# Splitting the first query/key stage, issuing stack slots singly, and a re-costed static schedule in a fused attention and mixture-of-experts layer

## The reference

```python
q, k, v = x @ Wq, x @ Wk, x @ Wv            # 16 heads of 8
q, k = rope(q), rope(k)
attn = softmax(where(causal, q @ k.T / sqrt(8), -inf)) @ v
x = layernorm(x + attn @ Wo)
# the experts: 8, of which each token takes the best 2; hidden width 256
rw, sel = top_k(x @ router_w.T + bias, 2);  rw = softmax(rw)
y = sum over the two of rw * (silu(x @ w1[e]) * (x @ w3[e])) @ w2[e]
y = y + (silu(x @ sw1) * (x @ sw3)) @ sw2   # the shared expert
out = layernorm(x + y)
```

## Time and profile before

| what | value |
|---|---|
| median of 3 runs | 689.45 us (682.46 to 692.08) |
| the profiled execution's own time | 689.81 us |
| its span | 687.8 us |
| mean granted TensorE clock | 0.885 of full |
| TensorE busy (matmul) | 545.5 us, 79% of the span |
| VectorE busy | 466.5 us, 68% |
| ScalarE, GpSimd busy | 317.6 us (46%), 321.1 us (47%) |

### The profile page before, as it was taken

One profiled execution on the slowest core, in us unless ns is written; L12 is line 12 of the kernel. 1 busy time (PEld: TensorE's weight loads), 2 busy tenths in 40 slices (PEclk: granted clock), 3 DMA queues, 4 the chain that ended last, 5 costly groups with the idle time before them and its releaser, 6 DMA issues.

```text
span 687.8 us, 14778 instructions
## 1 busy us (share of the span) xinstructions
PE 545.5 (79%) x4363; PEld 369.8 (54%) x4363; DVE 466.5 (68%) x1957; ACT 317.6 (46%) x771; POOL 321.1 (47%) x530
## 2 busy tenths in 40 slices
PE   5456888889787999987877979977978997777640
PEld 3111345347265757753555647754766876677640
DVE  3495899989676888756666998756577534753522
ACT  3103875665364676445633666336453582223220
POOL 4303733644871263277753363276462735552313
PEclk9765999999998999898987999897999999878885
DMA  5681322034227636352663536250756585538531
GB/s 150 173 267 42 102 72 71 3 118 125 92 84 220 194 102 194 94 173 80 185 157 116 151 98 193 75 173 28 210 155 188 170 230 151 153 102 249 178 114 40
DMA packets 80063, 94.09 MB, mean 137 GB/s; under 512 B 10224, under 2 KB 61168, under 8 KB 79984
## 3 DMA queue, kind: packets, MB, share of 16 engines
q1 hardware_dynamic: 75888, 84.75, 42.3%
q0 software_dynamic: 4096, 8.40, 3.7%
HBM read 70.37 MB, written 22.35 MB: 135 GB/s over the span
## 4 chain that ended last, share of the span: by engine, by line
PE 40%; DVE 15%; issue 12%; another core or an unknown queue 8%; DMA 7%; POOL 6%; SPq 6%; ACT 4%; POOLq 0%; DVEq 0%; ACTq 0%
PE ps L1099 11%; PE ps L1005 8%; PE ps L1111 6%; PE ps L961 6%; DVE sums L1178 4%; POOL yg L782 4%; SPq L650 3%; DMA parts_scratch<-parts 3%; ACT probs L824 2%; PE ps L947 2%; DVE gate L1303 2%; DVE acc L1321 2%; DMA rows_out<-y_routed 2%; PE ps L1083 1%
## 5 line engine op out<-in xcount | busy, mean ns | idle before, releaser
L1178 DVE CUSTOM_DVE_ANT_0 sums<-ps,mask_sb 128x384 bf16<-128x384 f32 (+3 forms) x512 | 218.9, 484 | 55.7 <-PE ps L961 36.0
L824 ACT ACTIVATE probs<-ps 128x512 f32<-128x512 f32 x320 | 171.8, 612 | 58.1 <-PE ps L961 45.4
L760 POOL TENSOR_SCALAR_AFFINE_SELECT probs<-probs 128x256 f32<-128x256 f32 (+1 forms) x320 | 112.8, 364 | 180.9 <-ACT probs L824 173.3
L961 PE MATMUL ps<-stack 64*128 64x512 bf16 (+3 forms) x1024 | 127.1, 323 | 46.3 <-DMA stack<-parts_scratch 14.4
L1099 PE MATMUL ps<-xgT,w_tile 128*128 128x128 f32 x792 | 116.9, 295 | 7.2 <-issue 6.8
L1303 DVE SCALAR_TENSOR_TENSOR gate<-th,ps 128x256 f32<-128x256 f32 x131 | 54.6, 417 | 93.7 <-ACT th L886 73.8
L1099 PEld LDWEIGHTS ps<-xgT,w_tile 128*128 128x128 f32 x792 | 104.4, 206 | 19.2 <-issue 14.9
L961 PEld LDWEIGHTS ps<-stack 64*128 64x128 bf16 x1024 | 43.1, 97 | 110.6 <-issue 29.1
L886 ACT ACTIVATE th<-ps 128x256 f32<-128x256 f32 x131 | 50.5, 388 | 93.0 <-PE ps L1099 72.4
L782 POOL DMA_INDIRECT yg<-rows_out,slot x64 | 61.2, 957 | 65.9 <-DMA rows_out<-y_routed 35.7
L1005 PE MATMUL ps<-probs,va 128*32 128x512 f32 (+3 forms) x1024 | 82.3, 465 | 6.5 <-POOL probs L760 5.3
(11 more groups left out here) (105 smaller groups left out, 597.2 us busy)
## 6 DMA issues: line engine op xcount, KB each, us to landing
w_tile<-in_experts SPq DMA_DIRECT2D x99, 384.0 KB
stack<-parts_scratch SPq DMA_DIRECT2D x112, 128.0 KB, 3.1
rows_out<-y_routed SPq DMA_DIRECT2D x99, 64.0 KB
parts_scratch<-parts SPq DMA_DIRECT2D x16, 384.0 KB, 3.6
xg<-rows_in SPq DMA_DIRECT2D x21, 256.0 KB
rows_in<-zeros SPq DMA_DIRECT2D x2, 1472.0 KB, 10.4
x_t<-in_x SPq DMA_DIRECT2D x8, 256.0 KB
x_r<-in_x SPq DMA_DIRECT2D x8, 256.0 KB
```

The lines of the kernel that those rows point to most:

```text
L760: pool.affine_select(out=area, in_=area, compare_op=ALU.is_ge, fill=0.0, base=0, pattern=pattern, channel_multiplier=-1).then_inc(masked, 1)
L824: act.activation(probs[:, (s * NB + v) % PRING, :], bank("scores", s, v), ACT.Exp, scale=SCALE)\
L961: return pe.matmul(into[:, at:at + width], here[:, stationary, at_s:at_s + P], here[:, moving, at_m:at_m + width], start=True, stop=True)
L1178: ins = dve.tensor_tensor_reduce(sums[:, use % 2, at:at + w], bank("max", s, u)[:, at:at + w], mask_sb[:, S - w:S], -1.0, 3.0e38, ALU.add, ...
```

## The change

- **Split by halves for sequence 0.** `rope_sum`, `split_high`, `split_rest`, `split_mid` and `split_low` run once for k and once for q (128x512 each, indices n = 0, 1). For the other sequences they run as before (n = 2). `store_parts(s, c)` is one transfer, placed by itself.
- **Stack slots as single parts.** Each of the seven transfers of a half is its own part in SP's list (`stack_slot`). For sequence 0 the slots with odd index are issued by ACT (`stack_first`), six in all. A `max_pair` still waits for all seven.
- **Start.** `load_x(0)` is issued ahead of the identity. VectorE sets a tile `idle` to zero, and TensorE runs WARM = 10 matmuls of 128x512 bf16 on it before its first part.
- **Durations.** Most entries of `COST` are new, with `SMALL` factors for small shapes, lengths of `count` and `rank` by group size, and other starting times of the engines in `plan()`.
- **Indirect DMAs.** In `plan()` a scatter or gather is placed at least `GAP` = 2600 ns after the one before it (1300 ns for the last group), and a TensorE result that would be ready within `HOLD` = 1000 ns of one is taken to be ready 100 ns after that.
- **TensorE's tiled mode.** In `plan()` a part that keeps the kind of tiling gets a bonus of 0.1 unit, and `SWITCH` is 180 ns instead of 200.
- **Rings.** `X1RING` 4 to 6, `ACCRING` 5 to 8.
- **Priorities.** Nearly all entries of `AT` and `LATER` are new, so the order of every engine changes.

```diff
-AT = dict(values=3.1, v=9.39, rows1=1.85, maxima1=11.32, heads_T0=1.6, heads_T1=4.56, out_T=7.38, out=-16.83,
...
-          stack0=-40.88, stack1=-17.63, rows0=-15.35, maxima0=-18.26, count=7.52, rank=11.17, scatter=14.65,
-          scatter_step=0.6, shared=12.71, shared_step=2.7, routed=33.25, margin=1.02, apart=0.95, T=-2.05, tanh=6.04,
-          glu=0.24, down=1.98, stored=5.64, weight_late=-0.8, gather=6.96, gather_step=2.43, combine=1.58,
-          lull_from=-6.91, lull_to=16.91, lull=1.64, routed_last_but_one=-0.14, routed_last=-2.57, apart_last=1.78,
-          gather_last=15.59, gather_step_last=0.35, combine_last=6.08)
...
+          rest=-46.59, low=-40.26, store_parts=5.53, stack0=-57.52, stack1=-22.66, rows0=-13.29, maxima0=-7.97,
+          count=-21.0, rank=6.22, scatter=17.87, scatter_step=0.06, shared=12.74, shared_step=2.41, routed=32.73,
+          margin=1.5, apart=0.36, T=-2.05, tanh=2.03, glu=0.68, down=1.08, stored=4.0, weight_late=7.4, gather=6.73,
+          gather_step=2.44, combine=-1.3, lull_from=-11.19, lull_to=16.8, lull=1.63, routed_last_but_one=-0.76,
+          routed_last=-11.25, apart_last=2.76, gather_last=17.6, gather_step_last=0.08, combine_last=-35.06)
...
-    pool=dict(rope=(2150, 2200), rest=(2150, 2200), low=(2150, 2200), scores=(400, 460), scatter=(980, 3000),
-              gather=(980, 3200), shared_rows=(440, 500), ln1=(1030, 1090), ln2=(1030, 1090)),
-    sp=dict(load_x=(430, 3100), load_residual=(430, 3100), store_parts=(900, 3300), stack=(3000, 5800), maxima=(1500, 3700),
...
+    pool=dict(rope=(2310, 2380), rest=(2090, 2160), low=(2090, 2160), scores=(365, 440), scatter=(1010, 4700),
+              gather=(1010, 4700), shared_rows=(415, 480), ln1=(1030, 1090), ln2=(1030, 1090)),
+    sp=dict(load_x=(500, 2900), load_residual=(500, 3800), store_parts=(700, 3700), stack=(635, 2900), maxima=(1800, 2950),
...
+GAP, GAP_LAST = 2600, 1300
+HOLD = 1000
+SWITCH = 180
...
-    X1RING, ACCRING = 4, 5
+    X1RING, ACCRING = 6, 8
...
+                if kind in ("scatter", "gather") and now < indirect + (GAP_LAST if part[2] == len(SORTED) - 1 else GAP):
+                    tries.append((indirect + (GAP_LAST if part[2] == len(SORTED) - 1 else GAP), engine))
                     continue
...
+            if kind in ("scatter", "gather"):
+                indirect = now
+            elif engine == "pe" and now + lasts < indirect + HOLD:
+                lasts = indirect + HOLD + 100 - now
...
+        def stack_slot(eng, s, half, k):
+            n = 2 * s + half
+            eng.wait_ge(scr_out, s * 32 + 32)
+            eng.wait_ge(flat_out, 16)
+            if n >= PLACES:
+                gone = n - PLACES
+                eng.wait_ge(*filled("scores", gone // 2, gone % 2 * (NB // 2) + NB // 2 - 1))
+            else:
+                eng.wait_ge(stack_p, n + 1)
+            qa, kb = SLOTS[k]
...
+            eng.dma_start(stack[k:P:DK, n % PLACES, :, :, :].rearrange("e c h n -> e c (h n)"),
+                          both_sides).then_inc(stacked[n % PLACES], 16)
...
-            def split_high(s):
+            def split_high(s, n):
                 if s > 0:
                     act.wait_ge(scr_out, s * 32)
-                act.wait_ge(qk_sb, s + 1)
-                act.activation(parts[:, :, 0, :], qk[:, :, :], ACT.Copy).then_inc(part0, 1)
...
+                act.wait_ge(qk_sb, split_count(s, n))
+                c = halves(n)
+                act.activation(parts[:, c, 0, :], qk[:, c, :], ACT.Copy).then_inc(part0, 1)
...
+            load_x(0)
             sp.dma_start(ident_sb[:, :], ident).then_inc(ident_in, 16)
-            load_x(0)
...
+            pe.wait_ge(idle_set, 1)
+            for n in range(WARM):
+                pe.matmul(ps[:, 7, :], idle[:, 0:P], idle[:, :], start=True, stop=True)
             pe.wait_ge(ident_in, 16)
...
+            dve.memset(idle[:, :].bitcast(F32), 0.0).then_inc(idle_set, 1)
```

More of the change, by code:

```diff
@@ L42 @@
[L42 to L56, removed]
@@ L147, in build_block @@
             add(now + AT[f"rows{half}"], "max_rows", s, half)
-            add(now + AT[f"stack{half}"], "stack", s, half)
+            for k in range(len(SLOTS)):
+                add(now + AT[f"stack{half}"] + 0.01 * k, "stack" if s or k % 2 == 0 else "stack_first", s, half, k)
             add(now + AT[f"maxima{half}"], "maxima", s, half)
@@ L357, in needs @@
         if kind == "store_parts":
-            return [low_of(s), ("sp", "stack", s - 1, 0), ("sp", "stack", s - 1, 1)]
+            own = [("dve", "low", s, key[1])] if s == 0 else split("low", s)
+            return own + [n for half in range(2) if s for n in stacked_by(s - 1, half)]
         if kind == "stack":
-            half = 2 * s + key[1] - PLACES
-            return [("sp", "store_parts", s, 0), ("pe", "score_pair", half // 2, 2 * NU * (half % 2) + 2 * NU - 1) if half >= 0 else None]
+            return stack_needs(s, key[1])
         if kind == "maxima":
@@ L379, in needs, with length @@
         return [("dve", "ln2", s)]
+    def length(part):
+        engine, kind, key = part[0], part[1], part[2:]
+        taken, lasts = COST[engine][kind]
+        if kind in ("count", "rank"):
+            taken, lasts = (round(t * (0.5 + 0.25 * len(SORTED[key[0]]))) for t in (taken, lasts))
+        if engine == "dve" and kind == "max" and key[1] % (2 * NU) < 4 or \
+                kind in ("rope", "rest", "low") and key[1] < 2:
+            taken, lasts = taken * SMALL[kind], lasts * SMALL[kind]
+        if part == ("sp", "load_x", 0, 0):
+            taken = FIRST_ISSUES
+        return round(taken), round(lasts)
     def plan():
@@ L417, in plan @@
                 part = found[-1]
-                if waits[part] or due[part] > now or best is not None and parts[best] <= parts[part]:
+                rank = parts[part]
+                if engine == "pe" and tiled == (kind in ("score_pair", "max_pair")):
+                    rank -= AT["stay"]
+                if waits[part] or due[part] > now or best is not None and first <= rank:
+                    continue
+                if kind in ("scatter", "gather") and now < indirect + (GAP_LAST if part[2] == len(SORTED) - 1 else GAP):
+                    tries.append((indirect + (GAP_LAST if part[2] == len(SORTED) - 1 else GAP), engine))
                     continue
```

195 lines of the change are left out of this document (116 added, 79 removed).

## The result

The changed kernel takes 651.38 us in the median of four runs (649.98 to 652.73), where the kernel before takes 689.85 on the same chip. The ratio is 0.9466, with an interval of 0.9401 to 0.9531, so it is 38.5 us faster. I had forecast 27. Its profiled execution has a span of 648.1 us.

The account below looks back on a forecast made before the run. TensorE, busy 79%, was nearest to a bound, with its signals held back by closely packed indirect DMAs. From 689.8 us, -5.0 for the head, -18 for spacing and -4 for single slots gave 663; range 638 to 688.

Parts of the forecast that it names:

- quiet stretches: Two stretches without trains of indirect DMAs, TensorE busy share times clock 0.82 and 0.88; moving over 0.03 would refute the prediction.
- the head: Serial start up to the first maxima matmul: warming, split, store and first stack together -5.0 us, bounds -8 to +1.5.
- the odd 8%: Chain share, some 55 us, put to another core or unknown queue; read as TensorE signals held back during indirect DMA issue.
- rival A: Spacing exists only in the plan and trains still form on the chip; 682 us, chance 0.22.
- the 5.24 us: ScalarE's idle time without a releaser before copying TensorE's values at 187.37 us, read as a signal held back by scatters.
- Indirect DMAs spaced, -18: Scatter and gather trains: three quarters of 24.3 us lost in five trains is regained; bounds -31 to 0.
- First stack: -1.3: Sequence 0's first seven slots, issued from SP and ACT, let the maxima matmul start 1.3 us earlier; bounds -1.9 to +0.5.
- The maxima behind the stack, 0: First half's maxima still wait behind sequence 1's slots on SP, so TensorE's 8.1 us idle stays; bounds -8 to 0.
- Single slots in SP's list, -4: Past the head, single slots let loads and stores between, removing most of 4.7 us of stack waits; bounds -8 to +15.
- rival C: Weight loads tear a half's slots apart on SP and delay stacks, making the kernel slower; 715 us, chance 0.08.
- Durations, tiled mode, priorities, 0: Every engine's new order, counted as nothing; bounds -14 to +14 us.
- The end stretch: From 617.2 us on, TensorE idle for 37 of 70.8 us; a change over 10 us would refute the prediction.

Follow-up runs that it names:

- e3: The changed kernel without the spacing rule in its planner (GAP and HOLD set to 0); ratio 0.9875 to the kernel before.
- e2: The kernel before with only the spacing rule added to its planner (2600 ns, 1300 in the last group, HOLD 1000); ratio 0.9628.
- e6: The changed kernel with the six sequence 0 stack slots that ACT issues given back to SP; ratio 0.9473.
- e9: The kernel before with every scatter and gather replaced by memsets on GpSimd that take as long; ratio 0.9546.
- e10: The changed kernel with every scatter and gather replaced by the same memsets on GpSimd; ratio 0.9399.
- e5: The changed kernel without the ten warming matmuls, all orders unchanged; ratio 0.9476.
- e7: The changed kernel with sequence 0's split steps made for k and q together again, all orders unchanged; ratio 0.951.
- e11: The changed kernel with the two zeroing transfers issued by SP behind the maxima of sequence 0's second half instead of behind its stack; ratio 0.9495.
- e8: The changed kernel with the priorities (AT and LATER) of the kernel before, all else kept; ratio 0.9707.
- e12: The kernel before with the spacing rule and the new durations, old priorities and none of the head's changes; ratio 0.99.
- e1: The kernel before with a GpSimd memset of about 0.9 us ahead of each of 96 scatters and gathers, orders unchanged; ratio 1.0798.

## Why the prediction was right or wrong, point by point

**Direction and size.** The time lies in the range, and the sign was right. The forecast of 27 us was 11.5 too small.

**A sign of being wrong that was met.** I had written that the prediction is wrong if the rate in quiet stretches moves by more than 0.03. It moved from 0.82 to 0.87 and from 0.88 to 0.93. The first of these lies ahead of all scatters, so spacing can't explain it. The first scatter starts at 159.4 us instead of 166.6, and without the spacing rule still at 160.5 (e3), but with the rule alone only at 165.2 (e2). So some 6 of those 7 us come from the other edits. My sum had 5 for the head and nothing for quiet stretches. How much of this lead reaches the end is not shown: in e6 the first scatter starts at 164.5 and the time is the same. The cause of the indirect DMAs stands all the same, by e2, e3, e9 and e10, but it was not the whole gain.

**The bound.** The reading of the odd 8% was right. TensorE's signals are held back by closely packed indirect DMAs (e2, e3, e9, e10), and the list's spacing makes real gaps in most places, so rival A (only the plan is spaced) did not happen as a whole. In places it did: 14 of 84 starts between 160 and 520 us are still closer than 1.6 us, and the longest delay that is left stands behind three such gathers.

The sentence on the earlier trace rows was too simple in two ways. Most of the 5.24 us was time in which TensorE was still at work. And the train is not made of scatters alone, since masks stand between many of them; the 0.30 us is the idle time between two that follow each other directly.

**Indirect DMAs spaced, -18.** The mechanism was right and the term was mis-sized. It measured 25 us when added to the kernel before (e2) and 28 us when removed from the changed one (4.1% of 690, e3). I had counted 24.3 us inside five trains and taken three quarters. Where the rest lies is not shown. The lower clock behind the trains and the other trains, which I had put into the outer bound (-31), are what was left to take it from.

**The head.** The first maxima matmul was forecast at 24 us and came at 27.21. Warming measured 1.2 against 1.3 (e5), and the split and the store together about 2.0 against 2.4 (e7). In the rows of the changed kernel q's low part is done at 16.30 and the slots begin 3.5 us later, where it was 3.7 from 18.78 to 22.50, so the store gave about 0.2 of its 0.4. The row at 15.73 holds both stores, k's at 15.73 and q's right behind q's low part. "First stack: -1.3" had the wrong sign: the matmul comes 7.42 us after the first issue against 6.55 before. With this the remark of the Trainium skill, "DMA: Bandwidth & Descriptors", section "Issuing engines are not separate DMA queues", that only the sequencer's time is saved, agrees with e6. My argument that 4.45 us of issue outweigh 2.1 of landing failed: the landing became the longer part. The gain of that edit lies elsewhere. SP is free 3.5 us sooner, and the queue behind it moves.

**The maxima behind the stack, 0.** This failed in size. The first score matmul came 6.3 us earlier (50.19 against 56.52) and the idle time before it fell from 8.1 to 4.8. As I wrote, the maxima still stand behind seven slots, but SP's whole queue came earlier. What of the head reaches the end stays open. Shifts of 3 us at the first scores in e6 and e11 moved the time by less than their intervals of about 0.6% each way can show, and in e11 the lead was gone by 105 us.

**Single slots in SP's list, -4.** Not tested by a run of its own. In the changed kernel's SP timeline most halves past the head are still issued seven in a row, in 4.4 to 5.9 us. A few are split, one into 2, 3 and 2 slots and one into 4 and 3, each over less than 8 us, so rival C had little to act on. TensorE's list of waits has no wait for `stack<-parts_scratch` past the head, where before it had 4.7 us. This is the list of the changed kernel:

```profile
PE ps L1036 <- DMA stack<-parts_scratch: 8.1, 1, 8.1
PE ps L1036 <- DMA stack<-mparts: 7.1, 3, 4.8
```

**Durations, tiled mode, priorities, 0.** The term was not 0. The priorities are worth 2.4%, some 17 us, beside the rest of the change (e8). New durations with old priorities cost 2.7%, some 19 us (e12 against e2). Each by itself is outside the bound of 14 us. The sum may be inside it, since all of the change but the indirect DMAs comes to 1.5%, some 10 us (e9, e10), but with the head and the slots in it. If the terms add at all, these are two large ones of opposite sign and not the small one that I had in mind. That the two were fitted to each other is likely. New priorities with old durations were not tried. The effect of the rings and of the bonus for tiled mode was not tried.

**The end stretch.** No change by more than 10 us was a condition, and in work it lost a little: 20 us of full-clock work in its last 70 us against 25. The gain is not there.

## What to carry to other kernels

If the chain shows waits with no releaser on a single core, look at what GpSimd issues at that time. Spread indirect DMAs through its list among work that waits for other engines by itself, and do not pad them with work of GpSimd's own. Test a cause by putting equal occupancy in its place, not by adding to it: the pause of e1 made the time worse for another reason, while the stand-in of e9 decided the question. Try new durations of a list scheduler together with new priorities: here truer durations under the old priorities made a worse schedule. And look at the signs of being wrong that you wrote down, even when the time came out in the range.

## What the runs showed of the hardware

- With scatters of 0.97 us, 0.30 us apart, there were up to 5.6 us between the end of TensorE's work and the copy that waited for it (459.53 to 465.10 in the kernel before). With memsets as dense in their place no wait without a releaser occurred (e9).
- The idle times without a releaser from 160 to 520 us came to 62.3 us with 47 of 80 starts of indirect DMAs less than 1.6 us behind the one before (kernel before) and to 64.8 with 60 of 85 (e3). They came to 13.0 with 14 of 84 (changed kernel), to 0.4 with 13 of 82 (e2), and to 0 where no start was closer than 2.07 us (e1).
- Seven transfers of 128 KB did not land sooner when issued from two queues (6.99 to 7.44 us to the first matmul in eight traces, against 6.55 to 6.95 from one queue in six), with the other seven under way at the same time.
- The kernel before took 663 to 690 us (medians) depending on the chip, so kernels from different chips can only be compared by ratio.
